# Chunked linear attention with sooner evictions and gates, and every second expert sum of two heads on GpSimd

## What is computed

```python
# first layer: 16 heads of 8 channels
v = (x @ Wv + bv); q = elu(x @ Wq + bq) + 1; k = elu(x @ Wk + bk) + 1
# scan over the tokens of a batch:
s = s + k_i (outer) v_i;  z = z + k_i
values_i = (q_i . s) / (q_i . z + 1e-6)
x = layernorm(x + values @ Wo + bo)
# second layer: H=8 heads, E=5 experts, DH=64, K=3
ss = sigmoid(x @ Ws); sd = sigmoid(x @ Wd)       # per token, head, expert
ms, md = topk_mask(ss, 3), topk_mask(sd, 3)
q = einsum('bthed,bthe->bhtd', x @ Wq, sd * md)   # a sum over the experts
k = einsum('bthed,bthe->bhtd', x @ Wk, ss * ms)
v = einsum('bthed,bthe->bhtd', x @ Wv, ss * ms)
out = softmax(q k^T * DH**-0.5) v
x = layernorm(x + (out @ Wo per expert, summed with md))
```

## Time and profile before

| what | value |
|---|---|
| median of 3 runs | 1871.56 us |
| profiled execution: its own time | 1867.74 us |
| its span, first to last instruction | 1865.9 us |
| first stage, until PE's first expert matmul | 227.4 us |
| busy: PE, DVE, ACT, POOL | 90%, 61%, 67%, 46% |
| mean granted clock of TensorE | 0.965 |

### The profile page before, as it was taken

How to read it: one execution, slowest core, us unless ns; L and a number is a source line. 1 busy time by engine, 2 the same in 40 slices (tenths; PEclk the granted TensorE clock), 3 DMA queues, 4 the chain that set the end, 5 groups by cost and what they waited for, 6 DMA issues and landing times. The chain is left out here.

```text
span 1865.9 us, 29217 instructions
## 1 busy us (share of the span) xinstructions
PE 1684.3 (90%) x10754; PEld 893.4 (48%) x10754; DVE 1137.7 (61%) x1948; ACT 1256.8 (67%) x2427; POOL 866.2 (46%) x575
## 2 busy tenths in 40 slices
PE   8888479999999999999999999779999999898975
PEld 4555356555565555655555555324233333332354
DVE  4666697997779886798876667431414223120196
ACT  4344115676776577675667676578899999999823
POOL 3355116787776688756787577850000000000033
PEclk9999699999999999999999999889999999999988
DMA  3000131221211121111112120230221312201001
GB/s 81 2 12 2 49 107 48 83 78 52 66 55 44 33 66 54 44 54 44 54 45 66 33 66 12 57 124 24 68 91 51 108 46 69 83 32 38 1 6 42
DMA packets 38790, 97.55 MB, mean 52 GB/s; under 512 B 5040, under 2 KB 16496, under 8 KB 38512
## 3 DMA queue, kind: packets, MB, share of 16 engines
q1 hardware_dynamic: 38640, 95.59, 16.5%
HBM read 49.96 MB, written 28.84 MB: 42 GB/s over the span
## 5 line engine op out<-in xcount | busy, mean ns | idle before, releaser
L1078 POOL TENSOR_TENSOR b_psum<-b_psum,b_probs 128x1024 f32<-128x1024 f32 x192 | 462.2, 2407 | 221.2 <-ACT b_probs L1220 214.9
L2511 ACT ACTIVATE c_probs<-banks 128x1024 f32<-128x1024 f32 x512 | 483.6, 1029 | 37.2 <-PE banks L2560 21.6
L1220 ACT ACTIVATE b_probs<-banks 128x1024 f32<-128x1024 f32 x256 | 255.5, 1020 | 231.1 <-PE banks L1360 230.3
L1325 PE MATMUL banks<-b_w,b_xh 128*128 128x480 f32 x1024 | 354.2, 398 | 33.2 <-issue 12.5
L1570 DVE TENSOR_TENSOR b_gated<-banks,b_g 128x480 f32<-128x480 f32 x512 | 310.6, 653 | 110.3 <-PE banks L1325 100.2
L1586 DVE TENSOR_REDUCE b_tok<-b_gated 128x192 f32<-128x960 f32 x256 | 281.5, 1138 | 0.5
L1189 ACT ACTIVATE b_share<-b_o,b_picked 128x64 f32<-128x64 f32 x1080 | 268.9, 340 | 1.7 <-DVE b_o L1611 1.7
L1395 PE MATMUL banks<-b_probs,b_tok 128*64 128x512 f32 x1024 | 252.1, 613 | 2.6 <-ACT b_probs L1220 2.6
L2574 PE MATMUL banks<-c_probs,c_vg 128*32 128x512 f32 x2048 | 249.7, 605 | 3.0 <-DVEq L2625 2.6
L1325 PEld LDWEIGHTS banks<-b_w,b_xh 128*128 128x128 f32 x1024 | 194.4, 190 | 116.5 <-issue 58.6
L1360 PE MATMUL banks<-b_qq,b_kk 64*128 64x512 f32 x1536 | 232.2, 426 | 5.0 <-DVE b_gated L1570 4.3
(11 more groups left out here) (265 smaller groups left out, 1814.3 us busy)
## 6 DMA issues: line engine op xcount, KB each, us to landing
b_w<-b_split_w SPq DMA_DIRECT2D x24, 960.0 KB, 4.7
b_kk<-b_kk SPq DMA_DIRECT2D x64, 256.0 KB, 3.7
c_heads<-c_split SPq DMA_DIRECT2D x24, 512.0 KB
c_keys<-c_heads SPq DMA_DIRECT2D x16, 512.0 KB, 3.8
c_queries<-c_heads SPq DMA_DIRECT2D x16, 512.0 KB, 4.7
b_split_w<-b_w SPq DMA_DIRECT2D x8, 960.0 KB, 6.1
b_raw_w<-in_L_ffn_W SPq DMA_DIRECT2D x8, 480.0 KB, 4.2
c_heads<-c_split SPq DMA_DIRECT2D x8, 384.0 KB
```

Source lines behind the costliest of these rows:

```text
L1078: nc.gpsimd.tensor_tensor(psum[:, par, :], prev, probs[:, i % 4, :], ALU.add).then_inc(psum_rdy, 1)
L1220: nc.scalar.activation(probs[:, i % 4, :], score_b[i % 2], ACT.Exp).then_inc(exp_rdy, 1)
L1325: last = nc.tensor.matmul(proj_b[u % WAYS][:, 0:HALF_W], a[:, x_of % 2, t * P:(t + 1) * P], w[:, par, part, j, :], start=(i == 0), stop=(i ...
L2511: nc.scalar.activation(probs[:, step % 4, c, :, :], unit_b[u % NU], ACT.Exp, scale=float(HD) ** -0.5).then_inc(exp_rdy, 1)
```

## The change

In the first stage the readers of pieces move up in their queues: on DVE `add_residual` of the batch before goes ahead of the masks, `take_values` goes directly behind them, and the norm's statistics are made one chunk sooner. On ACT the first `keep_apart` of a batch moves from chunk 5 to 4 and `finish_norm` is cut into two halves, at chunks 5 and 6. On POOL `inverse_roots` moves from chunk 5 to 4. In the last batch the second `gates` piece, `split_low`, and the clearing of `b_beats` come sooner, the latter writes the diagonal alone, more gate parts are done at each chunk, and the last norm takes the same way over DVE, POOL and ACT as the others. In the second stage POOL sums the experts of tiles 1, 3, 5 and 7 of the first two heads, by four dependent adds each. The old line numbers stand in the rows of before, new ones in those of the change.

```diff
     def zero_beats(self):
-        self.nc.gpsimd.memset(self.beats[:, :, :, :], 0.0).then_inc(self.clear, 1)
+        own = self.beats[:, :, :, :].rearrange("p c a b -> p c (a b)")[:, :, 0:self.E * self.E:self.E + 1]
+        self.nc.gpsimd.memset(own, 0.0).then_inc(self.clear, 1)
...
-                instead = {(1, 1): [("turn_next", b, 0)], (2, 1): [("turn_next", b, 1)], (3, 0): [("gates", b, 0)], (4, 0): [("gates", b, 1)]}
+                instead = {(1, 1): [("turn_next", b, 0)], (2, 1): [("turn_next", b, 1)], (3, 0): [("gates", b, 0)], (3, 1): [("gates", b, 1)], (4, 0): [("turn_share", b, 0)]}
...
-                    if c == 5 and b:
+                    if c == 4 and b:
                         inverse_roots(b - 1)
...
-                    if c == 5 and b + 1 == B:
+                    if c == 3 and b + 1 == B:
                         pool.wait_ge(qk_rdy, 4 * B)
                         front.zero_beats()
+            inverse_roots(B - 1)
...
-            def finish_norm(b):
+            def finish_norm(b, half):
 
                 act.wait_ge(newton, NEWTON_STEPS * (b + 1))
-                for t in range(NT):
+                for t in range(4 * half, 4 * half + 4):
...
-                    if b + 1 < B and c in (5, 7):
+                    if b + 1 < B and c in (4, 7):
                         keep_apart(b + 1, c // 7)
...
-                    if c == 6 and b:
-                        finish_norm(b - 1)
+                    if c in (5, 6) and b:
+                        finish_norm(b - 1, c - 5)
+            for half in range(2):
+                finish_norm(B - 1, half)
...
                     n = b * NT + c
+                    if c == 0 and b:
+                        add_residual(b - 1, 0)
                     if n + 1 < CHUNKS:
                         mask_scores(n + 1)
+                    if c == 0:
+                        take_values(b, 1)
+                    if c == 6 and b + 1 < B:
+                        take_values(b + 1, 0)
                     if c < NT - 1:
                         keep_state(n)
-                    if c == 0:
-                        if b:
-                            add_residual(b - 1, 0)
-                            values(b - 1, 1)
-                        take_values(b, 1)
+                    if c == 0 and b:
+                        values(b - 1, 1)
                     if c == 1 and b:
                         add_residual(b - 1, 1)
+                        norm = moment_parts(b - 1)
+                        next(norm)
                     if c == 2:
                         shares(b)
-                        if b:
-                            norm = moment_parts(b - 1)
-                            next(norm)
-                    if c in (3, 4) and b:
+                    if c in (2, 3) and b:
                         next(norm)
...
+                    if c == 3 and b == B - 1:
+                        front.split_low(dve, 0)
                     if c == 4 and b == B - 1:
-                        front.split_low(dve, 0)
                         dve.wait_ge(*reads(index["gates", b, 1]))
                         dve.wait_ge(front.clear, 1)
                         gates = front.gate_parts(dve, 0)
                     if c >= 4 and b == B - 1:
-                        next(gates)
-                        next(gates)
+                        for _ in range((3, 3, 4, 4)[c - 4]):
+                            next(gates)
             values(B - 1, 1)
-            for _ in range(6):
-                next(gates)
             add_residual(B - 1, 0)
             next(gates)
-            next(gates)
-            dve.wait_ge(newton, NEWTON_STEPS * (B - 1))
             add_residual(B - 1, 1)
-            dve.wait_ge(*reads(index["project", B - 1, 1]))
-            st = Steps(dve, norm_steps)
-            layer_norm(nc, st, y, out[:, (B - 1) * NT:B * NT, :], stats, mv, rs, tmp)
-            st.settle()
+            norm = moment_parts(B - 1)
+            for _ in norm:
+                pass
             for _ in gates:
                 pass
...
+            def sum_aside(n, t):
+
+                pool.wait_ge(mult, MULT0 + U * n + 2 * t + 2)
+                dst = tok[:, n % 4, :, t, :].rearrange("p j (f d) -> p f j d", f=2)
+                part = gated[:, t % 2, :, :].rearrange("p f (j d e) -> p f j d e", j=3, e=E)
+                done = (E - 2) * (NT // 2 * n + t // 2)
+                nc.gpsimd.tensor_tensor(dst, part[:, :, :, :, 0], part[:, :, :, :, 1], ALU.add).then_inc(side_step, 1)
+                for e in range(2, E):
+                    pool.wait_ge(side_step, done + e - 1)
+                    nc.gpsimd.tensor_tensor(dst, dst, part[:, :, :, :, e], ALU.add).then_inc(side_step if e < E - 1 else tok_side, 1)
+
-            for n in range(2 if ready else 0, 3):
+            for n in range(0 if not ready else 2, 2):
                 front.low_weights(pool, n, n % 2)
+            for n in range(2):
+                for t in range(1, NT, 2):
+                    sum_aside(n, t)
+                if n == 0:
+                    front.low_weights(pool, 2, 0)
...
             def turn_keys(n):
 
-                pe.wait_ge(tok_rdy, TOK0 + NT * (n + 1))
+                pe.wait_ge(tok_rdy, TOK0 + NT * max(n + 1, 2))
...
             def gate_part(n, b, h, t, j):
 
-                if j == 0:
+                if j == 0 and n < 2:
+                    if t % 2:
+                        dve.wait_ge(tok_side, NT // 2 * n + t // 2)
+                    else:
+                        dve.wait_ge(tok_rdy, TOK0 + NT // 2 * n + t // 2)
+                elif j == 0:
...
-                    sum_experts(n, t)
+                    if t % 2 == 0:
+                        sum_experts(n, t)
+            dve.wait_ge(tok_side, NT)
+            dve.sem_inc(tok_rdy, NT)
```

More of the change, by code:

```diff
@@ L353, in linear_into @@
         taken, masked_last = map(sem, ("taken", "masked_last"))
-        share_rdy, vals_rdy, xb_rdy, moments, newton, normed, norm_steps = map(sem, ("share", "vals", "xb", "moments", "newton", "normed", "norm_steps"))
+        share_rdy, vals_rdy, xb_rdy, moments, newton, normed = map(sem, ("share", "vals", "xb", "moments", "newton", "normed"))
         MASKED = NG - 1
@@ L851, in _ @@
                         values(b, 0)
-                        if b + 1 < B:
-                            take_values(b + 1, 0)
                     if c == 7 and b + 1 < B:
                         running_sum(b + 1)
+                    if c == 3 and b == B - 1:
+                        front.split_low(dve, 0)
                     if c == 4 and b == B - 1:
-                        front.split_low(dve, 0)
                         dve.wait_ge(*reads(index["gates", b, 1]))
@@ L936, in switch_attention @@
         xT_ps, xT_sb, gate_ps, gate_exp = map(sem, ("xT_ps", "xT_sb", "gate_ps", "gate_exp"))
-        proj_ps, mult, tok_rdy = map(sem, ("proj_ps", "mult", "tok_rdy"))
+        proj_ps, mult, tok_rdy, tok_side, side_step = map(sem, ("proj_ps", "mult", "tok_rdy", "tok_side", "side_step"))
         turn_ps, high_rdy, k_low, q_low = map(sem, ("turn_ps", "high", "k_low", "q_low"))
```

## The result

| what | before | after |
|---|---|---|
| median, all runs made together | 1871.26 us (4 runs, 1869.36 to 1872.44) | 1841.07 us (4 runs, 1836.85 to 1842.83) |
| ratio, with its 95% interval | | 0.9836 (0.9818 to 0.9855) |
| profiled execution: own time, span | 1867.74, 1865.9 us | 1842.83, 1840.9 us |
| first stage, until PE's first expert matmul | 227.37 us | 198.65 us |
| from there to `low_keys` | 39.37 us | 41.27 us |

A forecast was written before the change was run, and what follows sets the result against it. Waits at first-stage seams and the last batch's end, from queue order, and DVE's pace in the expert heads bound it. 20.2 + 8.6 - 0.3 = 28.5 us off the 1871.56 median gives 1843; range 1838 to 1854.

The forecast's parts named there:

- The seams: Three boundaries between first-stage batches: reordered queues shorten PE's waits, 6.0, 7.5 and 6.7 us, sum 20.2.
- (1): Third seam, ACT: four `a_apart` copies go one chunk earlier, ahead of the exp that `spread` awaits; costs 1.4 us.
- (2): Third seam, DVE: `a_v` read straight behind the masks, so the second `spread` starts at 150.5 instead of 152.07.
- (4): Third seam, DVE: scan starts at 154.6, `a_y` read next; PE's `v` starts near 158.0 instead of 163.89.
- (3): Third seam, ACT: only four norm activations before `a_kt`, so `project` starts at 155.7 instead of 158.84.
- Rival (b): ACT binds the seams: early `a_apart` copies push other work, each seam gains only 3 us; 1854 us, chance 0.10.
- The last batch: First stage's end: gates 8.5 us sooner, 0.4 from a mask reduction moved, -0.3 for the ending; sum 8.6 us.
- The ending: Last norm handed from DVE to POOL's roots (3.9 us) and ACT's activations (3.2), 7.4 with hand-overs against 7.1: -0.3.
- The expert heads: First two second-stage heads: DVE loses eight reductions but waits for GpSimd; `low_keys` at 267.1 against 266.74, 0.3 us lost.
- S: GpSimd's sum of one tile, four dependent adds of 0.60 us: 2.63 us; `low_keys` starts at 246.0 + 8 S.
- Rival (a): Strided GpSimd adds are dearer, 0.79 us each, S = 3.4: 6.5 us lost instead of 0.3; 1849 us, chance 0.32.
- (d): DVE holds GpSimd's expert sums off, 2.3 us an add, S 9.4: slower than before, 1897 us; chance 0.03.

The follow-up runs named there:

- packed adds: The changed kernel with GpSimd adds reading 32 neighbouring elements instead of every fifth (wrong sums, only durations meant): `low_keys` 38.79 us behind the first expert matmul; its 8931 us measure nothing.
- 26.0 in the second: The changed kernel measured again, five rounds on one chip, against the kernel before (1867.22 us, 15 runs): 1841.20 us, ratio 0.9863.

## Why the prediction was right

**The seams** (predicted 20.2 with the first one's slow scores): 5.63, 7.76 and 6.85 us against 5.4, 7.5 and 6.7, and 0.66 for those scores against 0.6; 20.9 in all. Taking DVE's order back gives up 18 of it, ACT's 1.8. By its steps: (1) `spread` waits 1.63 us for the exp, 1.3 more than before, as the 1.4 said; (2) and (4) hold, the waits for `a_v` and `a_y` are gone; (3) holds, with 1.13 us of wait for `a_kt` left: `project` starts 20.94 us behind the third seam's first scores, forecast 21.05 (155.7 - 134.65). Rival (b) had the right mechanism and a fraction of its size: the early copies cost some 1 us a seam and gain nothing. But the seam that all this is measured against is not the same in every execution: the first one took 31.49 us in the profile of before, and 32.96 and 33.39 in the runs with the clear moved and with the sums alone, which are the same program up to there (granted clock 0.86 instead of 0.91). Against those the first seam gains 7.1 to 7.5, not 5.6.

**The last batch** (8.6): 7.8. The gates came 8.68 us sooner (8.5). The mask reduction moved behind the statistics (+0.4) brought -0.57, mostly by two things: DVE is held 1.2 us at 172.92 by POOL's mask and waits 1.27 instead of 0.44 us for PE's last projection; statistics start 20.54 us behind the gates instead of 19.97. The ending took 0.34 more from there (-0.3): roots 4.48 instead of 3.9 us, since five of the steps last 0.29 to 0.33 instead of 0.20 once DVE's gate arithmetic runs beside them. The clear took 1.82 us and not the 0.6 of "the old rate"; it was hidden, so this error cost nothing.

Start 0.05, seams and slow scores 20.90, last batch 7.77: 28.72 us, the whole way from 227.37 to 198.65.

**The expert heads** (-0.3): -1.9. The formula held to 0.9 us: with the measured S of 2.94 us (204.49 to 207.43), 246.0 + 8 S is 269.5, and the measured place, carried to the old start, 227.37 + 41.27 = 268.6. With the packed adds, S was the 2.63 that I took, and `low_keys` came at 38.79 where the formula has 39.7, again 0.9 sooner; most of that is the cycle, S + 1.33 and not S + 1.41. The mis-sized term is S: in-place adds of 0.69 instead of 0.60 us. Rival (a), that the step costs, had the right mechanism and twice its size (0.79), that of GpSimd held off by DVE, (d), did not happen: 24 adds within 683 to 702 ns, beside products and reductions. Its turning point is a slip: S = 6.2 is 1.49 us an add, not 1.55, since the hand-overs between the adds are part of S.

**The sum**: 28.7 - 1.9 = 26.8 us by place, 28.5 predicted: 1.7 too much. The medians differ by 30.2 in the first comparison and by 26.0 in the second, and the two profiled executions by 24.9. So it is partly luck that 1843 lies only 1.9 from 1841.07: the sum was too high for the places of these two profiles, and the executions of before vary by more than that. Some of it lies in later stages that the change left alone (1594.3 against 1587.8 us with the same program), some in the first stage of before, whose third seam ends at 168.13 us in the profile, and at 170.74 and 170.68 in the two other runs named above.

## What to carry to other kernels

Where many readers share one bank, put the read that frees it ahead of everything in its queue that nobody waits for yet; and test each moved item alone, because in a good set one may work against the rest (here the early query copies). Work handed to a slower engine is worth no more than its consumer's wait lets through: the same sums lost 2 us with one wait for both heads and gained 2.9 with a wait for the head that was needed. The end of a stage is a place where the engine that has just finished can take half of the last job.

## What the runs showed of the hardware

Some DVE and POOL instructions block each other for their whole length. Beside a clear of 1.82 us an 8-element DVE instruction lasted 1.83 instead of 0.17, beside one of 2.77 us 2.77; a 512-element comparison was held until POOL's mask ended; and at 141.19 us four POOL copies took 3.01 us beside DVE's scan, which had itself started beside POOL's subtraction (139.01 to 141.25) and took 3.02 us; in the run with DVE's old order it started just behind the end of that subtraction and took 2.35. Others do not: DVE's products with one operand in PSUM and its reductions were not held by 32 adds, nor held them, and two reciprocals (2.17 us at 166.72) ran beside POOL's root steps, which stayed at 0.20. The Trainium skill (SBUF — State Buffer, Who interferes with whom) gives the same picture: one exclusive, shared port pair, the first to start keeps it for its whole instruction. The rows of the change agree; in the run with DVE's old order the copies are recorded 0.09 us ahead of the scan (155.51 and 155.60), and still it is they that took 2.99 us. Nor is a clear priced by its elements alone: 640 with a step took 1.82 us, 3200 side by side 2.77.
